# Attention scores with 288 contraction rows taken as 128 + 128 + 32, and queries laid out through DRAM

## What is computed

```
B, q_len, s_len = 2, 512, 1024 + 512      # keys and values of context and latents
H, KV, HD, G = 16, 4, 96, 4               # 4 query heads share a key head
q = (latents @ Wq.T)   k = (hidden @ Wk.T)   v = (hidden @ Wv.T)
scores = einsum('bkgqd,bksd->bkgqs', q, k) / sqrt(96)
out = einsum('bkgqs,bksd->bkgqd', softmax(scores), v)
x = x + tanh(g) * (out @ Wo.T)
```

## Time and profile before

| | us |
|---|---|
| median of 3 runs | 1117.86 (1116.97 to 1121.5) |
| the profiled execution, its own time | 1116.84 |
| its span, first to last instruction | 1115.0 |

### The profile page before, as it was taken

How to read it: one execution, slowest core, us unless ns; L and a number is a source line. 1 busy time by engine, 2 the same in 40 slices (tenths; PEclk the granted TensorE clock), 3 DMA queues, 4 the chain that set the end, 5 groups by cost and what they waited for, 6 DMA issues and landing times.

```text
span 1115.0 us, 18666 instructions
## 1 busy us (share of the span) xinstructions
PE 1057.9 (95%) x7315; PEld 592.5 (53%) x7315; DVE 620.1 (56%) x1091; ACT 628.3 (56%) x700; POOL 605.0 (54%) x303
## 2 busy tenths in 40 slices
PE   6999999999999998999999999999999999987985
PEld 2555534444454555555656655665655655654552
DVE  7773738754312455555655654654654654677665
ACT  4674643442212666655666756656765567676743
POOL 4313535533100478855767855668855658675741
PEclk9999999999999999999999999999999999998996
DMA  9652673573214899999999999999999999998983
GB/s 349 222 210 74 207 260 123 115 141 62 43 54 131 184 199 218 195 209 185 183 191 210 189 203 195 185 203 201 191 197 199 175 197 186 167 171 154 182 179 113
DMA packets 513621, 196.65 MB, mean 176 GB/s; under 512 B 479194, under 2 KB 494170, under 8 KB 513538
## 3 DMA queue, kind: packets, MB, share of 16 engines
q1 hardware_dynamic: 513538, 195.52, 84.4%
HBM read 56.72 MB, written 13.63 MB: 63 GB/s over the span
## 4 chain that ended last, share of the span: by engine, by line
PE 75%; DMA 7%; DVE 5%; ACT 4%; POOL 3%; SPq 3%; issue 2%; DVEq 0%; POOLq 0%; ACTq 0%
PE ps L528 33%; PE ps L730 16%; PE ps L745 9%; PE ps L704 9%; PE ps L747 4%; DMA region_o<-region_y 3%; POOL region_y L1561 3%; DMA region_c<-region_b 2%; ACT region_b L1148 1%; DVE p_max L1412 1%; PE ps L631 1%; PE ps L604 1%; SPq L491 1%; SPq L487 1%; ACT p L1138 1%
## 5 line engine op out<-in xcount | busy, mean ns | idle before, releaser
L1561 POOL TENSOR_TENSOR region_y<-p,region_b 128x1536 f16<-128x1536 f32 x128 | 396.9, 3101 | 296.8 <-ACT region_b L1148 239.1
L1412 DVE TENSOR_REDUCE p_max<-ps 128x1 f32<-128x1536 f32 x128 | 224.9, 1757 | 129.5 <-PE ps L730 129.5
L1138 ACT ACTIVATE p<-ps,p_max 128x1536 f32<-128x1536 f32 x128 | 197.0, 1539 | 170.4 <-DVE p_max L1412 170.1
L730 PE MATMUL ps<-region_q,region_c 96*128 96x512 f16 x1152 | 270.0, 379 | 0.8 <-DMA region_c<-region_q 0.8
L1148 ACT ACTIVATE region_b<-ps,p_max 128x1536 f16<-128x1536 f32 x128 | 196.6, 1536 | 66.7 <-DMA region_c<-region_b 66.5
L745 PE MATMUL ps<-region_q,region_c 128*128 128x192 f16 x1536 | 209.4, 248 | 13.4 <-DMA region_o<-region_y 10.4
L747 PE MATMUL ps<-region_q,region_o 128*128 128x96 f16 x1536 | 204.1, 207 | 0.0
L745 PEld LDWEIGHTS ps<-region_q,region_c 128*128 128x128 f16 x1536 | 151.0, 98 | 35.4 <-issue 18.6
L730 PEld LDWEIGHTS ps<-region_q,region_c 96*128 96x128 f16 x1152 | 105.4, 98 | 108.8 <-issue 1.4
L747 PEld LDWEIGHTS ps<-region_q,region_o 128*128 128x128 f16 x1536 | 151.0, 98 | 11.9 <-issue 0.3
L528 PE MATMUL ps<-region_w,region_q 128*128 128x512 f16 x576 | 136.5, 383 | 2.9 <-POOL region_w L1561 1.1
(11 more groups left out here) (119 smaller groups left out, 1063.7 us busy)
## 6 DMA issues: line engine op xcount, KB each, us to landing
stage<-ctx_t_in SPq DMA_DIRECT2D x16, 512.0 KB, 5.5
stage<-ctx_in SPq DMA_DIRECT2D x16, 512.0 KB, 4.6
stage<-wq_in SPq DMA_DIRECT2D x16, 384.0 KB, 4.1
stage<-wo_in SPq DMA_DIRECT2D x16, 384.0 KB, 4.5
k_scratch<-region_o SPq DMA_DIRECT2D x12, 384.0 KB, 5.9
region_q<-k_scratch SPq DMA_DIRECT2D x8, 576.0 KB, 6.0
region_q<-v_scratch SPq DMA_DIRECT2D x8, 576.0 KB, 6.3
x_res<-x_in SPq DMA_DIRECT2D x8, 512.0 KB, 11.8
```

The source lines that it names most:

```text
L730: ins = nc.tensor.matmul(bank(NSB * (m % 2) + sb_), q_head[0:HD, b, h, hq, qt * P:(qt + 1) * P], k_head[0:HD, b, hk, sb_ * 512:(sb_ + 1) * ...
L1138: nc.scalar.activation(p32[:, m % 2, :], rows, ACT.Exp, bias=p_max[:, m % 4:m % 4 + 1], accum_out=den[:, m % 4:m % 4 + 1]).then_inc(e32_ok, 1)
L1412: nc.vector.reduce_max(p_max[:, m % 4:m % 4 + 1], rows, axis=AX, negate=True).then_inc(max_ok, 1)
L1561: return nc.gpsimd.tensor_tensor(out, a, b, op)
```

## The change

Scores: the 288 rows are taken as 128 (96 of HI·HI, with 32 of HI·LO), 128 (96 of LO·HI, with the next 32 of HI·LO) and 32 (the last of HI·LO). The third set of keys is kept in `k_rest`, where rows 0 to 31, 32 to 63 and 64 to 95 hold the three blocks of 512 keys, so that the three matmuls with 32 rows each use another group of rows of the array and another PSUM bank. The queries must then stand in partitions 96 to 127 and in three copies as well, so they go to DRAM (`q_dram`) and are loaded from there.

```
-PT = 4
+PT = 3
+HP = HD // 3
 def load_k(t):
-    sp.dma_start(k_head[0:HD, b, :, :], src).then_inc(k_ld[b], 16)
+    for n in range(2):
+        sp.dma_start(k_head[0:HD, b, n, :], rows[HI]).then_inc(k_ld[b], 16)
+        sp.dma_start(k_head[HD:P, b, n, :], rows[LO, n * HP:(n + 1) * HP, :]).then_inc(k_ld[b], 16)
+def load_k_rest(t):
+    for s in range(NSB):
+        sp.dma_start(k_rest[HP * s:HP * (s + 1), b, :], last[:, s * 512:(s + 1) * 512]).then_inc(k_ld[b], 16)
-def load_q(t, j):            # per block j: two DMAs, q_blk to q_head
+def store_q(t, j):
+    sp.wait_ge(q_free, NJ * t + j + 1)
+    sp.dma_start(q_dram[t % B, j * P:(j + 1) * P, :, :], q_blk[:, j, :, :]).then_inc(q_st, 16)
+def load_q(t):
+    sp.wait_ge(q_st, 16 * NJ * (t + 1))
+    sp.dma_start(q_head[0:HD, b, :, 0:2, :], heads).then_inc(q_ld[b], 16)
+    for n in range(2):
+        sp.dma_start(q_head[HD:P, b, :, n, :], heads[n * HP:(n + 1) * HP, :, HI, :]).then_inc(q_ld[b], 16)
+    for s in range(NSB):
+        sp.dma_start(q_head[HP * s:HP * (s + 1), b, :, 2, :], heads[2 * HP:HD, :, HI, :]).then_inc(q_ld[b], 16)
 # ahead of the loop
-for j in range(NJ): load_q(0, j)
+for j in range(NJ): store_q(0, j)
+load_q(0)
+load_k_rest(0)
 # in the loop; load_k is followed by load_k_rest
 if q_end(m) is not None:
-    load_q(t + 1, q_end(m))
+    store_q(t + 1, q_end(m))
+if m > 0 and q_end(m - 1) == NJ - 1:
+    load_q(t + 1)
 # scores(m)
-for n, (hq, hk) in enumerate(((HI, HI), (HI, LO), (LO, HI))):
-    for sb_ in range(NSB):      # q_head[0:HD, b, h, hq, tok], k_head[0:HD, b, hk, 512 columns]
+for n in range(2):
+    for s in range(NSB):
+        nc.tensor.matmul(bank(NSB * (m % 2) + s), q_head[:, b, h, n, tok],
+                         k_head[:, b, n, s * 512:(s + 1) * 512], start=n == 0, stop=False)
+for s in range(NSB):
+    rows = slice(HP * s, HP * (s + 1))
+    ins = nc.tensor.matmul(bank(NSB * (m % 2) + s), q_head[rows, b, h, 2, tok], k_rest[rows, b, :],
+                           start=False, stop=True)
-V_AT = {0: 2, 1: 3}
+V_AT = {0: 3}                  # the value product of tile 2 is made ahead of the loop
```

More of the change, by code:

```diff
@@ L73, in flamingo @@
         p32 = sb("p32", [P, 2, SL], F32)
+        o_tok = sb("o_tok", [P, 2, QG], F32)
         def view(region, start, n, dt=F16):
@@ L94, in flamingo, with turned_p @@
         w_eff = view(region_c, 0, 16384).rearrange("p (h c n) -> p h c n", h=2, c=NC)
[L96 to L99, removed]
+        q_head = view(region_c, 0, 12288).rearrange("p (b g x s) -> p b g x s", b=2, g=G, x=3)
+        k_rest = view(region_c, 12288 + 2 * SL, 2 * 512).rearrange("p (b s) -> p b s", b=2)
+        def turned_p(region, start):
+            return view(region, start, SL).rearrange("p (n q) -> p n q", n=NS)
+        pt_hi = [turned_p(region_c, 12288), turned_p(region_c, 12288 + SL), turned_p(region_o, 3 * SL)]
+        pt_lo = [turned_p(region_o, r * SL) for r in range(PT)]
         p_hi = region_b[:, 0:SL].bitcast(F16).rearrange("p (r s) -> p r s", r=2)
@@ L172, in flamingo @@
         k_dram = nc.dram_tensor("k_scratch", (B, 2, KVD, SL), F16).ap()
+        q_dram = nc.dram_tensor("q_scratch", (B, QG, 2, QL), F16).ap()
         v_dram = nc.dram_tensor("v_scratch", (B, KV, P, NS, VW), F16).ap()
@@ L404, in load_k @@
                 g, b = t // B, t % B
-                src = k_dram[b, :, g * HD:(g + 1) * HD, :].rearrange("h d s -> d h s")
-                sp.dma_start(k_head[0:HD, b, :, :], src).then_inc(k_ld[b], 16)
+                rows = k_dram[b, :, g * HD:(g + 1) * HD, :]
+                for n in range(2):
+                    sp.dma_start(k_head[0:HD, b, n, :], rows[HI]).then_inc(k_ld[b], 16)
+                    sp.dma_start(k_head[HD:P, b, n, :], rows[LO, n * HP:(n + 1) * HP, :]).then_inc(k_ld[b], 16)
+            def load_k_rest(t):
+                g, b = t // B, t % B
+                last = k_dram[b, LO, g * HD + 2 * HP:(g + 1) * HD, :]
+                for s in range(NSB):
+                    sp.dma_start(k_rest[HP * s:HP * (s + 1), b, :], last[:, s * 512:(s + 1) * 512]).then_inc(k_ld[b], 16)
             def load_v(t):
@@ L411, in load_v @@
                 sp.dma_start(v_head[:, b, :, :].rearrange("p s w -> p (s w)"), src).then_inc(v_ld[b], 16)
-            def load_q(t, j):
+            def store_q(t, j):
                 sp.wait_ge(q_free, NJ * t + j + 1)
[L415 to L421, removed]
+                sp.dma_start(q_dram[t % B, j * P:(j + 1) * P, :, :], q_blk[:, j, :, :]).then_inc(q_st, 16)
+            def load_q(t):
+                b = t % B
+                sp.wait_ge(q_st, 16 * NJ * (t + 1))
+                heads = q_dram[b].rearrange("(g d) h s -> d g h s", g=G)
+                sp.dma_start(q_head[0:HD, b, :, 0:2, :], heads).then_inc(q_ld[b], 16)
+                for n in range(2):
+                    sp.dma_start(q_head[HD:P, b, :, n, :], heads[n * HP:(n + 1) * HP, :, HI, :]).then_inc(q_ld[b], 16)
+                for s in range(NSB):
+                    sp.dma_start(q_head[HP * s:HP * (s + 1), b, :, 2, :], heads[2 * HP:HD, :, HI, :]
+                                 ).then_inc(q_ld[b], 16)
             def turn(n, i):
@@ L451, in _ @@
             for j in range(NJ):
-                load_q(0, j)
-            sp.wait_ge(v_lo_ok, 5 * 4 + 2)
-            sp.dma_start(v_dram[1].rearrange("k p s w -> p k s w")[:, :, CTX // P:CTX // P + 2, :], v_out[:, :, 0:2, :]
+                store_q(0, j)
+            load_q(0)
+            load_k_rest(0)
+            sp.wait_ge(v_lo_ok, 5 * 4 + 3)
+            sp.dma_start(v_dram[1].rearrange("k p s w -> p k s w")[:, :, CTX // P:NS - 1, :], v_out[:, :, 0:3, :]
                          ).then_inc(v4_st, 16)
@@ L486, in _ @@
                 sp.wait_ge(exp_ok, m + 1)
-                sp.dma_start_transpose(pt_hi[:, m % PT, :, :], p_hi[:, m % 2, :]).then_inc(pt_hi_ld[m % PT], 16)
+                sp.dma_start_transpose(pt_hi[m % PT], p_hi[:, m % 2, :]).then_inc(pt_hi_ld[m % PT], 16)
                 if m == NU - 1:
@@ L498, in _ @@
                     load_k(1)
+                    load_k_rest(1)
                     load_v(1)
@@ L502, in _ @@
                     load_k(t + 1)
+                    load_k_rest(t + 1)
                     load_v(t + 1)
                 if q_end(m) is not None:
-                    if t > 0 and q_end(m) == 0:
+                    store_q(t + 1, q_end(m))
+                if m > 0 and q_end(m - 1) == NJ - 1:
+                    if t > 0:
                         sp.wait_ge(sc_ready, UPS * t)
-                    load_q(t + 1, q_end(m))
+                    load_q(t + 1)
                 if t % 2 == 0 and u in WQ_LOAD and t < TS - 2:
@@ L682, in value_product @@
             def value_product(at, tt):
-                pe.wait_ge(v_lo_ok, 5 * 4 + tt - 1 if tt < 2 else 5 * 4 + tt)
+                pe.wait_ge(v_lo_ok, 5 * 4 + tt - 1 if tt < 3 else 5 * 4 + tt)
                 for c in range(NC):
@@ L723, in scores @@
                 if u == 0:
-                    pe.wait_ge(k_ld[b], use(t, B))
+                    pe.wait_ge(k_ld[b], 7 * use(t, B))
                     pe.wait_ge(q_ld[b], 6 * use(t, B))
@@ L727, in scores @@
                     pe.wait_ge(exp_ok, m - 1)
-                for n, (hq, hk) in enumerate(((HI, HI), (HI, LO), (LO, HI))):
-                    for sb_ in range(NSB):
-                        ins = nc.tensor.matmul(bank(NSB * (m % 2) + sb_), q_head[0:HD, b, h, hq, qt * P:(qt + 1) * P],
-                                               k_head[0:HD, b, hk, sb_ * 512:(sb_ + 1) * 512], start=n == 0, stop=n == 2)
+                tok = slice(qt * P, (qt + 1) * P)
+                for n in range(2):
[6 more added lines that the diff above has]
+                                           start=False, stop=True)
                 ins.then_inc(sc_ready, 1)
@@ L744, in weigh @@
                 for i in range(NS):
-                    nc.tensor.matmul(bank(6, VW), pt_hi[:, m % PT, i, :], v_head[:, b, i, :],
+                    nc.tensor.matmul(bank(6, VW), pt_hi[m % PT][:, i, :], v_head[:, b, i, :],
                                      start=i == 0, stop=False, skip_group_check=True)
-                    ins = nc.tensor.matmul(bank(6, HD), pt_lo[:, m % PT, i, :], v_head[:, b, i, 0:HD],
+                    ins = nc.tensor.matmul(bank(6, HD), pt_lo[m % PT][:, i, :], v_head[:, b, i, 0:HD],
                                            start=False, stop=i == NS - 1, skip_group_check=True)
@@ L757, in _ @@
             value_product(4, 1)
+            value_product(3, 2)
             def router(at, i):
@@ L784, in side_free @@
                 if 0 < m < UPS:
-                    pe.wait_ge(v_lo_ok, 5 * 4 + 2 + sum(v in V_AT for v in before))
+                    pe.wait_ge(v_lo_ok, 5 * 4 + 3 + sum(v in V_AT for v in before))
                 pe.wait_ge(q_free, NJ + sum(q_end(v) is not None for v in before))
@@ L795, in _ @@
                 if m == 1:
-                    pe.wait_ge(v_lo_ok, 5 * 4 + 2)
```

(8 more changed lines are left out.)

8 lines of the change are left out of this document (4 added, 4 removed).

## The result

The changed kernel takes 1163.97 us in the median (1163.64 to 1170.1), 46.6 us more than the kernel before, run beside it (1117.41): ratio 1.042, 95% interval 1.039 to 1.044. The forecast was 1139, some 21 us more than before, with a range of 1098 to 1172. The direction and the range held; the forecast slowdown was less than half of what came.

The account below looks back on a forecast made before the run. PE (99%) and SP's DMA queue (97%) were taken as both full, the queue deciding. Span 1115.0 + 22 (34 prices less 12 slack) + 2.5 start - 3 end = 1136.5 us; median 2.9 above: 1139, range 1098 to 1172.

Parts of the forecast that it names:

- What binds: In the attention loop PE (99%) and SP's DMA queue (97%) are full at once; the queue decides after the change.
- PE's saving: Scores of a unit take seven matmul times instead of nine: 0.43 us less a unit, 55 in 128 units.
- The slack: SP's gaps in the seven turns, 17.3 us, mostly close once PE is faster: 12 us taken off.
- The queue's prices: Added loop DMAs, priced by distances between high transposes: +4.8 us a turn (0.1 to 15.5), +34 in seven turns.
- the value product's 4.1: PE makes the value product 4.06 us earlier, at the start; moved only, so it comes back in units 0 and 1.
- the keys and values: Loop loads of a turn, 7 key DMAs instead of 1: 5.6 us against 4.5 before, +1.1 (+0.5 to +4).
- the three stores: Query stores to DRAM in each turn, 0.262 MB each: 3.0 us a turn together (2.0 to 6.3).
- The start: Ahead of the loop, a store, loads and their landing delay the first scores to 367.7 from 365.2 us: +2.5 (0 to +6).
- The end: In the last turn, where the queue carries no loads, about half of PE's 6.9 us saving shows: -3 (0 to -7).
- The third buffer: Wait for `pv_ok` before high transposes, with three buffers instead of four: 0 us.
- The stores' wait: `load_q` on SP waits for the query stores to land, holding everything behind it: 0, at most 2 us a turn.
- The late queries: Rival: query loads land after a turn's scores could begin; PE stands 2 to 4 us a turn; 1160 to 1200, chance 0.11.

Follow-up runs that it names:

- Experiment 1: The kernel before with 7 instead of 9 score matmuls in a unit, its DMAs unchanged: 1112.08 us, 0.994 to the kernel before.
- experiment 2: The changed kernel with all its DMAs, but scores made by nine matmuls of 96 rows: 1165.72 us, 1.0425 to the kernel before.
- 5: Kernel before and changed kernel, most loop loads and query stores cut to one partition, same DMA count: 1110.09 and 1110.88 us, both 0.993 to the kernel before.
- pe7_only: The same run as Experiment 1: the kernel before with 7 instead of 9 score matmuls in a unit, 1112.08 us, 0.994.

## Why the prediction was right in its direction and short in its size

- **What binds: right.** Two full resources, and the change decided by the queue. Experiments 1, 2 and 5 show both halves.
- **PE's saving: mis-sized.** 0.23 us a unit, not 0.43 (1.71 us against 1.94), 29 us in all. The mode change that TensorEngine Tiling (Key Properties) in the Trainium skill says to drain TensorE is seen here as 0.1 us either way. I had set the rule aside. It made nothing of the result, because PE's time was off the path: with all of its work given back (experiment 2) the time moved by 2 us.
- **The slack: a step that failed.** I took 12 of SP's 17.3 us of gaps as free. Experiment 1 shows 3.3 (by its medians up to 6.7), though its gaps did close by 11.9: the rest came back as longer holds of SP. So the gaps of the issuing engine could not be counted as free time. That the DMA engines work off a backlog in the gaps is my reading of this; the runs show the holds.
- **The queue's prices: the other step that failed, too low.** +34 for seven turns, 4.8 a turn. Against the turns with PE's saving alone (610.5) the change adds 39.5 us, or 43.6 if the value product's 4.1 came back in them; turns 1 to 6 alone give 6.3 a turn. By distances between high transposes in the changed kernel (taken as in the prediction) the keys and values cost about 6.1 us a turn (I said 5.6), the three stores 4.5 (3.0), the query loads 6.8 (7.0); less the 10.8 of before that is +6.6. The term most in error is the store to DRAM: 1.5 us each, not 1.0. And I had summed keys and values to +1.1 where they added 1.6.
- **The start: short by 2.2.** +8.8 against +6.6 ahead of the first high transpose. The first scores came at 368.7 us, 1.0 later than forecast. I gave the last loads the 2.8 us of a copy from SBUF to SBUF; loads from DRAM landed in 5.3 to 5.7 us (`k_rest`) and 5.6 to 6.1 (queries). That it cost so little is luck: the last store had landed at 359.6, 2 us before I thought. After the wait the first scores ran at half clock and took 3.2 us, where the nine of before took 1.9. The moved value product does seem to come back in turn 0, as I had it. The first scores of the changed kernel:

```profile
368.69 2.72 PE L757 MATMUL ps<-region_q,region_c 128*128 128x512 f16 x6 [5.07 <-DMA region_c<-k_scratch]
371.34 0.60 PE L761 MATMUL ps<-region_c 32*128 32x512 f16 x3
```

- **The end: wrong by 4.8.** -3 against +1.8, in pe7_only +1.5. With less PE work the last turn and tail were no shorter in any of these kernels. Why is not tested; it is made of waits between all engines.
- **Waits.** The third buffer cost nothing, as forecast. The stores' wait cost nothing that a run singles out. The late queries were right at the edge.

The misses on prices (9.6), slack (8.7), start (2.2) and end (4.8) are the 25.3 us between 1136.5 and 1161.8. The split of the first two can shift by some 3 us, by what one takes from experiment 1. If the value product did not come back in the turns, 4.1 of the 9.6 are that, and not prices.

## What to carry to other kernels

When one engine is 99% busy, look at who else has no gaps: order the issuing engine's rows by time, and if each starts where the last ended, price every added DMA by the distance between two recurring ones, before counting what the busy engine saves. Don't count the issuing engine's gaps as slack; ask what the DMA engines do in them. And a saving in one of two full resources is worth little until the other is relieved: here 55 us of PE's work gave 6, and with next to no bytes in the queue the change still won only 13 us in its turns.

## What the runs showed of the hardware

- Three matmuls with 32 rows in three row groups and three banks start 3 ns apart and take the time of one; in one row group they take 0.216 us each. Going to them from full matmuls and back costs about 0.1 us each way, in one row group as well (706.99 and 707.74 us above).
- Behind a full queue, a query load of 128 KB (32 partitions) took 6.0 us to land in the median, one of 768 KB (96 partitions) 6.1; the SBUF-to-SBUF copies of 192 KB took 2.8.
- After PE had waited 3.94 us ahead of a turn, its matmuls ran at half clock (granted 0.5, so 1.2 instead of 2.4 GHz); after a wait of 3.78 us ahead of another turn it kept 2.4 GHz. The length of the wait alone does not tell: ahead of turn 6 the clock fell after one of 2.50 us (granted 0.56 from 924.52 to 926.50 us). The first six score matmuls after the waits of 3.78 and 3.94 us, in the changed kernel:

```profile
643.39 1.46 PE L757 MATMUL ps<-region_q,region_c 128*128 128x512 f16 x6 [3.78 <-issue]
...
736.51 2.24 PE L757 MATMUL ps<-region_q,region_c 128*128 128x512 f16 x6 [3.94 <-issue]
```
